# A head's products with the values in front of the turning of the next head, in both attention loops of a decoder layer

## The reference

```
# cross attention
scores = jnp.einsum('bhqd,bhkd->bhqk', qh, kh) + attn_mask
probs = jax.nn.softmax(scores, axis=-1)
ctx = jnp.einsum('bhqk,bhkd->bhqd', probs, vh)
# causal attention
scores = jnp.einsum('bhqd,bhkd->bhqk', q, k) / jnp.sqrt(jnp.float32(HEAD_DIM))
scores = jnp.where(causal, scores, -jnp.inf)
attn = jax.nn.softmax(scores, axis=-1)
out = jnp.einsum('bhqk,bhkd->bhqd', attn, v)
# the layer
x = x + _L0_attn_ref(_layernorm(x, axis=-1), ...)
x = x + _L0_xattn_ref(_layernorm(x, axis=-1), ctx_1024, ctx_1024, fside_Bx1xSxS2_0, ...)
x = x + _L0_ffn_ref(_layernorm(x, axis=-1), ...)
```

## Time and profile before

| | us |
|---|---|
| median of 3 runs (1405.01 to 1407.26) | 1405.26 |
| the profiled execution, as a whole | 1409.84 |
| its span, first to last instruction | 1408.0 |
| PE busy in the span (89%) | 1253.5 |
| DVE busy (68%) | 954.2 |
| ACT busy (48%) | 677.8 |
| POOL busy (19%) | 268.9 |

### The profile page before, as it was taken

The page is one execution under the profiler, slowest core; times in us unless marked ns, Lnnn a source line. Parts: engine busy times, 40 slices in busy tenths (PEclk is TensorE's granted clock), DMA queues, the critical chain, the costliest instruction groups (busy, mean ns, idle before and its releaser), DMA issues. The chain is left out here.

```text
span 1408.0 us, 25262 instructions
## 1 busy us (share of the span) xinstructions
PE 1253.5 (89%) x8404; PEld 1110.5 (79%) x8404; DVE 954.2 (68%) x2934; ACT 677.8 (48%) x1527; POOL 268.9 (19%) x282
## 2 busy tenths in 40 slices
PE   5889998999899898989999899899994369999997
PEld 4668988867799796769988877799894258888886
DVE  6867767776576687666767676576777955555553
ACT  3727627563564474536627563564574113333332
POOL 2001005110000431000015010000433313333332
PEclk9999999999999999999999999999996569999999
DMA  6026400010551001026400010651701002222221
GB/s 246 1 51 140 110 17 1 1 61 0 138 125 38 16 2 61 1 67 140 94 16 1 25 37 0 144 128 30 284 2 32 1 17 37 38 39 39 38 38 24
DMA packets 45661, 80.38 MB, mean 57 GB/s; under 512 B 8448, under 2 KB 18176, under 8 KB 45024
## 3 DMA queue, kind: packets, MB, share of 16 engines
q1 hardware_dynamic: 37376, 69.19, 18.2%
q0 software_dynamic: 6720, 9.18, 4.0%
q10 hardware_dynamic: 1440, 0.39, 0.1%
HBM read 28.01 MB, written 8.78 MB: 26 GB/s over the span
## 5 line engine op out<-in xcount | busy, mean ns | idle before, releaser
L1036 ACT ACTIVATE b_pp<-b_pp,b_nm 128x256 f32<-128x256 f32 x256 | 116.0, 501 | 83.6 <-DVE b_nm L1074 82.6
L912 PEld LDWEIGHTS bank<-b_va,b_pt 128*128 128x128 f32 x1024 | 128.8, 193 | 4.4
L912 PE MATMUL bank<-b_va,b_pt 128*128 128x65 f32 x1024 | 129.3, 270 | 0.0
L1371 PE MATMUL bank<-c_v,c_pt 128*128 128x68 f32 x768 | 102.1, 269 | 4.0 <-DVE c_pt L1597 3.5
L1371 PEld LDWEIGHTS bank<-c_v,c_pt 128*128 128x128 f32 x768 | 97.2, 191 | 7.8 <-DVE c_pt L1597 7.0
L1074 DVE CUSTOM_DVE_ANT_0 b_pp<-bank,mask 128x256 f32<-128x256 f32 x256 | 96.9, 417 | 0.0
L1878 ACT ACTIVATE e_th<-bank 128x512 f32<-128x512 f32 x35 | 21.0, 601 | 146.4 <-PE bank L102 146.4
L100 PE MATMUL bank<-e_up_low,e_xh 128*128 x210 | 89.7, 427 | 1.8 <-DVE e_xl L208 1.8
L197 PE MATMUL bank<-identr 128*128 128x512 f32 x274 | 76.2, 429 | 14.9 <-DVE a_cv L617 8.2
L1349 PE MATMUL bank<-c_kv,c_qv 128*128 128x128 f32 (+1 forms) x512 | 89.2, 298 | 0.0
L1589 DVE CUSTOM_DVE_ANT_0 c_pp<-bank,const 128x128 f32<-128x128 f32 (+1 forms) x256 | 80.0, 350 | 11.3 <-PE bank L1349 10.8
(11 more groups left out here) (403 smaller groups left out, 3673.4 us busy)
## 6 DMA issues: line engine op xcount, KB each, us to landing
b_kst<-b_kh SPq DMA_DIRECT2D x128, 128.0 KB, 2.3
k_low_twice<-b_kl SPq DMA_DIRECT2D x128, 128.0 KB, 2.4
b_qst<-b_ql SPq DMA_DIRECT2D x64, 128.0 KB, 2.4
raw_up<-in_w SPq DMA_DIRECT2D x4, 768.0 KB, 10.0
raw_down<-in_w SPq DMA_DIRECT2D x4, 768.0 KB, 12.1
XN<-in_x SPq DMA_DIRECT2D x5, 512.0 KB, 4.5
context<-in_ctxT SPq DMA_DIRECT2D x4, 512.0 KB, 5.9
mask<-in_mask SPq DMA_DIRECT2D x4, 512.0 KB, 6.7
```

The lines of the kernel that those rows point to most:

```text
L912: ins = pe.matmul(O2[u % 2][:, at:at + VW], pt[:, n % 2, kt * S + qt * P:kt * S + (qt + 1) * P], va[:, b * QT + kt, 2 * j + hp, :], start= ...
L1036: act.activation(pp[:, n % 3, qt, :], pp[:, n % 3, qt, :], ACT.Exp, bias=nm[:, n % 4, qt:qt + 1], scale=-1.0).then_inc(s["probs_exp"], 1)
L1371: ins = pe.matmul(OB[u % 2][:, at:at + AKV * AVW], pt[:, n % 4, i * P:(i + 1) * P], v[:, b * QT + kt].rearrange("p a b -> p (a b)"), start ...
```

## The change

In both loops the call of `values(n - 1)` moves up, from behind `turn(n)` and the projection or build to the place between `scores(n + 2)` and `turn(n)`. Nothing else is changed; the same instructions run with the same waits, and the other engines' queues stay as they are.

```diff
             for n in range(NHD + 1):
                 if n + 2 < NHD:
                     scores(n + 2)
+                if n >= 1:
+                    values(n - 1)
                 if n < NHD:
                     turn(n)
                 if next_projection(n):
                     project(*next_projection(n))
-                if n >= 1:
-                    values(n - 1)
...
             for n in range(NHD + 1):
                 if n + 2 < NHD:
                     scores(n + 2)
+                if n >= 1:
+                    values(n - 1)
                 if n < NHD:
                     turn(n)
 
                 if n % PER in (0, 2, 4) and n // PER + 1 < AKV:
                     build(3 * (n // PER) + n % PER // 2)
-                if n >= 1:
-                    values(n - 1)
```

## The result

| | before | after |
|---|---|---|
| median | 1405.45 (1405.01 to 1407.26) | 1487.22 (1482.65 to 1488.97) |
| the profiled execution, as a whole | 1409.84 | 1487.91 |
| its span | 1408.0 | 1486.1 |
| four cross loops, first T to last H | 300.16 | 349.89 |
| four causal loops, first T to first output product | 204.89 | 238.44 |

The ratio of the medians is 1.0574 (95% interval 1.0548 to 1.06): 82 us slower, where the prediction had 73. The loops grew by 49.7 and 33.6 us, 83.3 together; the rest of the span became 5.2 us shorter, 3.6 of it in the stages ahead of a cross loop and 1.6 behind the last causal one.

The account below looks back on a forecast made before the run. PE's queue was taken to bound both loops; uncovered handovers from T to V add 11.2 us per cross loop and 7.0 per causal loop, four passes of 18.2 making 73 us on 1405.3: 1478 us, range 1455 to 1506.

Parts of the forecast that it names:

- (b): Cross loop, even heads behind a projection: pairs +0.77 us with queries, +0.42 with keys; 6.7 us per pass.
- (c): Cross loop, heads without a projection: 23, 25, 27 cost 1.5 us together, 0 and 24 cost 0.8; 26 all but covered.
- (d): Cross loop's end, no S left as cover: S(31) to the last H 8.40 us instead of 6.20, +2.2 per pass.
- Head 0: Cross loop's start: V waits for ACT's copy, 2.23 us instead of 1.81, 0.42 per pass.
- Odd heads: Causal loop, only S as cover: 1.81 us instead of 1.47, +0.34 for each of thirteen, 4.4 us per pass.
- Even heads with a build of L1321: Causal loop: cover of 1.17 us against a handover of 1.05, so no cost.
- Heads 6, 14 and 24: Causal loop, even heads without build or four transposes: 0.27 us each, 0.8 per pass.
- The end: Causal loop, S(31) to the first output product: 6.85 us instead of 5.09, +1.8 per pass.
- S did not hide the copy: Rival, both loops: S(n+2) hides the copy and V never waits; at most a win to 1392 us; chance 5%.
- Rival 2: Even V waits for mask, exponentials and copy in a row; 58 us over the cross loops, 1536 us; chance 6%.
- Rival 3: Changed loops: recurring gaps drop PE's clock to the 1.2 GHz level; +125 us, 1603 at most; chance 3%.
- The lower one: Both loops: waiting Vs pay no extra 0.13 or 0.10 us; 18 us less, 1460 us.

Follow-up runs that it names:

- half of it: V(n-1) moved in front of T(n) only for the even heads, in both loops, against the kernel before: 1461.39 us, ratio 1.0395.
- the longer copies: Changed kernel plus an extra unread 256-column copy on ACT ahead of each of its copies, in both loops: 1533.78 to 1575.32 us in four runs.

## Why the prediction was right, and where a term was mis-sized

- **V waits for the copies** in both loops, with ACT's and DVE's copies as releasers, 19 times per cross loop and 21 per causal loop; T no longer waits for the exponentials inside a loop; a V behind a P does not wait. As predicted.
- **(b) Pairs with a projection:** 5.78 and 5.40, predicted 5.78 and 5.43. **(c):** the handover by DVE 1.39 against 1.38; heads without P take 2.34 (170.81 to 173.15) and 2.23 (to 175.38), predicted 2.32 and 2.23. **(d):** S(31) at 184.02 to H at 192.60 is 8.58, predicted 8.40.
- **Head 0** is the term of the cross loop that was mis-sized: 0.42 per pass, where the start grew by 6.75 - 5.34 = 1.41. I had looked for the clock in the middle of the loops, and had not read the start of a pass. The wait itself was right, 0.39 with the clock at 1.00; the other 1.0 is the lower clock, which the term did not have. A cross loop became 12.4 us longer, predicted 11.2: of the 1.2, 1.0 is the start and 0.2 the end.
- **Causal loop:** 8.4 per pass, predicted 7.0. Odd heads take 1.14 + 0.72 (232.21 to 232.93) = 1.86 instead of 1.81, thirteen times 0.05 = 0.65. Even heads with a build of L1321 are not free: cover 1.07 (232.93 to 234.00) is met by the handover of 1.05, but V then starts from idle too, 0.73 to the next T, about 0.1 on each of six = 0.6. Heads 6, 14 and 24 wait for ACT as predicted, 1.07 from T to V against 1.05. The end takes 7.04 (281.79 to 288.83), predicted 6.85, 0.2. The sum, 1.45, is about the miss.
- **Rivals.** S did not hide the copy. Rival 2 is absent in the whole change; half of it shows that chain. Rival 3 holds at one place, the start of the cross loop, for about 1.0 us per pass more than before, and not behind it. Its own sign, a granted clock under 1.00 in the loops, was there: 0.98 in the first cross loop, all of it from the start.
- **Bounds.** The lower one, with no extra for a V that starts from idle, was wrong: every V that waited at full clock paid it (0.94 and 0.72 to the next T). The terms missing in the sum, 2.6 us per pass, make 10 of the 83 us in the loops.

## What to carry to other kernels

When a result goes from one engine to another and back, count in the new order what is left between the producing and the consuming step of the same head; the handover (transposes, copy, semaphores: 1.07 to 1.39 us here) must fit into it, and swapping two steps shortens that distance even if neither is lengthened. Moving one of two alternating consumers can be free or even a gain while moving both is not, so test the halves. Read the first iteration of a loop by itself, with its granted clock.

## What the runs showed of the hardware

**A low clock at a loop's start.** Ahead of T(0) PE is idle for 1.81 us, waiting for the first exponentials, and the granted clock behind it is 0.50 to 1.00, from pass to pass of one execution. With eight products in that gap 1.00 was granted in all eight passes of the two kernels that have them, and the changed kernel's start had one length in all four. They cost nothing that shows. The idle time is not the whole of it: in the fourth pass of after 0.50 was granted already from 951.0 to 953.4 us, ahead of T(0) at 953.5, and PE's wait there is 1.24 us; what took the clock down there stays open.

**Many short waits did not take the clock down.** In the middle of the first cross loop of after V waits 14 times for 0.2 to 0.6 us, and 1.00 is granted throughout; with the longer copies it fell to 0.50 at the loop's end, where no S stands between the waits any more. It fell there also in one pass of the kernel with the even heads moved (9.67 us for 9.02 from S(31) to H) and in one of the changed kernel with PE kept busy (9.19 for 8.59).

```profile
115.00:185.00 70.00, 64.76 (x487) 59.12 (x488) 47.50 (x178) 43.52 (x88) 8.14 (x5) 1.00 0.43 99
```

The Trainium skill (TensorE: Matmul & The Clock Gate, A second HAM failure mode: psum-queue depth-cycling) tells of a kernel whose clock went back and forth because PE idled briefly between its groups of products. By that rule the clock would have moved in the middle of these loops too; this row disagrees there, and the end of the loop with the longer copies (0.50) agrees.

**A V that starts from idle** is shown at 1.11 us instead of 1.00 and puts off the next group by 0.13 us in the cross loop; this part of a wait stands under busy time.
